# Decoder kernel: the first attention block in three-pass products with filler projections, and a new order of loading

## The reference

```
y = layernorm(layernorm(x)) * g1 + b1
q, k, v = y @ Wq + bq, y @ Wk + bk, y @ Wv + bv        # 256 -> 1024 each
g = sigmoid(y @ Wg + bg)
state_t = decay * state_(t-1) + k_t * v_t               # a scan over the 100 rows
o = (g * q * state * 64**-0.5) @ Wo + bo                # 1024 -> 256
x2 = layernorm(x) + o
h = layernorm(x2) * g2 + b2
x = x + x2 + gelu(h @ W1 + b1) @ W2 + b2                # 256 -> 1024 -> 256
```

## Time and profile before

| what | us |
|---|---|
| median of 3 runs (1713.19 to 1713.71) | 1713.41 |
| the profiled execution | 1713.2 |
| its span, first to last instruction | 1711.4 |
| PE busy | 1443.1 (84%) |
| VectorE busy | 1041.3 (61%) |
| ScalarE busy | 736.7 (43%) |
| POOL busy | 33.6 (2%) |
| mean granted TensorE clock | 0.927 |

### The profile page before, as it was taken

One profiled execution on the slowest core, in us unless ns is written; L12 is line 12 of the kernel. 1 busy time (PEld: TensorE's weight loads), 2 busy tenths in 40 slices (PEclk: granted clock), 3 DMA queues, 4 the chain that ended last, 5 costly groups with the idle time before them and its releaser, 6 DMA issues.

```text
span 1711.4 us, 26949 instructions
## 1 busy us (share of the span) xinstructions
PE 1443.1 (84%) x9474; PEld 1143.6 (67%) x9474; DVE 1041.3 (61%) x2519; ACT 736.7 (43%) x1919; POOL 33.6 (2%) x31
## 2 busy tenths in 40 slices
PE   0498989898799999999999999843899995997608
PEld 0355656565588787888888888632788885677608
DVE  4843434334466666666666666578566765687784
ACT  0322122222366555565555655510444533443744
POOL 1000000000100000000000000000000002000100
PEclk9899999999899999999999999966799996998858
DMA  9120000000000000000000000001100000220001
GB/s 298 30 99 1 0 0 0 0 0 0 17 10 10 19 10 9 9 9 9 9 9 9 9 9 1 1 0 27 43 1 0 0 0 0 73 72 1 1 0 39
DMA packets 29797, 35.56 MB, mean 21 GB/s; under 512 B 5119, under 2 KB 26928, under 8 KB 29744
## 3 DMA queue, kind: packets, MB, share of 16 engines
q1 hardware_dynamic: 27840, 27.53, 5.5%
q0 software_dynamic: 1904, 7.34, 1.3%
HBM read 33.20 MB, written 1.65 MB: 20 GB/s over the span
## 4 chain that ended last, share of the span: by engine, by line
PE 72%; DVE 17%; ACT 5%; issue 4%; DMA 1%; SPq 0%; DVEq 0%; ACTq 0%
PE bank L624 10%; PE bank L659 8%; PE bank L660 7%; PE bank L661 7%; PE bank L721 5%; PE bank L705 5%; PE bank L713 4%; PE bank L632 3%; PE bank L681 3%; PE bank L650 3%; PE bank L642 3%; PE bank L851 2%; PE bank L875 2%; ACT s L1297 2%; DVE amax L1832 2%
## 5 line engine op out<-in xcount | busy, mean ns | idle before, releaser
L1218 ACT ACTIVATE prob<-bank,nmx 100x361 f32<-100x361 f32 x256 | 142.5, 560 | 124.6 <-DVE nmx L1633 124.6
L1633 DVE TENSOR_REDUCE nmx<-bank 100x1 f32<-100x361 f32 x256 | 124.7, 528 | 44.7 <-PE bank L705 33.8
L1589 DVE TENSOR_TENSOR oTl<-bank,oTh 128x100 fp32r<-128x100 f32 x128 | 33.3, 260 | 120.1 <-ACT oTh L1204 120.1
L659 PE MATMUL bank<-cxTh,wxkh 128*128 128x362 f32 x256 | 99.1, 387 | 0.8 <-DVE kTl L1590 0.6
L721 PE MATMUL bank<-pT,vv 128*64 128x100 f32 (+1 forms) x1536 | 95.5, 260 | 0.7 <-DVE oTl L1589 0.7
L1650 DVE TENSOR_SCALAR prob<-prob,rsum 100x361 f32<-100x361 f32 x256 | 92.9, 405 | 4.5
L721 PEld LDWEIGHTS bank<-pT,vv 128*64 128x64 f32 (+1 forms) x1536 | 70.3, 138 | 35.8 <-issue 23.1
L713 PE MATMUL bank<-ident,prob 100*128 100x100 f32 (+1 forms) x768 | 89.7, 253 | 1.9 <-DVE prob L1650 1.9
L713 PEld LDWEIGHTS bank<-ident,prob 100*128 100x128 f32 (+1 forms) x768 | 84.5, 151 | 7.2 <-DVE prob L1650 2.7
L1204 ACT CAST oTh<-bank 128x100 fp32r<-128x100 f32 x128 | 31.7, 248 | 128.6 <-PE bank L721 128.6
L659 PE MATMUL bank<-wxvh,cxTh 128*128 128x512 f32 (+1 forms) x192 | 83.7, 436 | 1.0 <-DVE vv L1618 1.0
(11 more groups left out here) (342 smaller groups left out, 3598.8 us busy)
## 6 DMA issues: line engine op xcount, KB each, us to landing
cx<-in_ctx_dram SPq DMA_DIRECT2D x32, 128.0 KB, 2.1
xc<-in_ctx_dram SPq DMA_DIRECT2D x32, 128.0 KB
mask_i<-in_mask_BxS_ik_dram SPq DMA_DIRECT2D x16, 141.0 KB
w<-in_L_attn_W_dram POOLq DMA_DIRECT2D x2, 1024.0 KB, 26.9
cx<-in_ctx_dram SPq DMA_DIRECT2D x16, 105.0 KB, 2.1
xc<-in_ctx_dram SPq DMA_DIRECT2D x16, 105.0 KB
x<-in_x_dram SPq DMA_DIRECT2D x1, 1600.0 KB
out_dram<-x SPq DMA_DIRECT2D x8, 200.0 KB
```

The source lines that it names most:

```text
L659: pe.matmul(o, wh, mh, start=start, stop=False)
L1218: nc.scalar.activation(prob[:, h % 4, :], bank[S_BANKS[e]][0:T, 0:S], ACT.Exp, bias=nmx[:, h:h + 1], accum_out=psum_[:, h:h + 1]).then_inc ...
L1633: nc.vector.tensor_reduce(nmx[:, h:h + 1], bank[S_BANKS[e]][0:T, 0:S], AX_X, ALU.max, negate=True).then_inc(xa_max, 1)
```

## The change

*Loading.* SP issues x by groups of four, the four projection weights by halves of 512 columns in the order k, g, v, q, then Wo, W1, W2 and two raw weights. ScalarE's queue issues the identity, the vectors and the small ones. POOL issues no DMA any more. Later raw weights go into the same two buffers (`raw6`, `raw2`) as these come free.

*First norms.* The second of two norms without gain has the same mean, so `u0` is made from x with one factor, `rstd_z`, that is worked out from the first variance; first for group 0, the others within group 0's chunks.

*Products.* All seven weights of the block are split in high (ScalarE) and low (VectorE); POOL does both for the second halves of k, g, v, q. Rows, heads and hidden values are split too: y and h by ScalarE (whole and high) and POOL or VectorE (low), heads and gelu outputs by POOL. All products are `split_matmul`. Wo and W2 now give the transposed sum: the weights are stationary, each chunk is added to banks 4 and 5 as soon as it is split, ScalarE copies the sum with its bias, and PE transposes it back (`sums_back`). k, g, v and q have one bank each.

*Filler.* While a group's end runs, PE makes the first three chunks of the next group. `transposes(u0, SIDE_BANK0, l0_t)`, those of the second norm, stand ahead of the whole third of them.

*Side jobs.* The weight transposes of the head, and the rounding, are spread over the groups (`JOBS_AT`). The transposed FFN weights are written to HBM (`parked`) and loaded back when the 4-bit layer is done.

The loop over groups is written out. The core of the diff, PE first:

```diff
-            with pe.Fori(0, NG) as g:
-                for c in range(KC):
-                    p = 4 * (c % 2)
...
-                    for w, b in ((wk0, 1), (wg0, 3), (wv0, 2), (wq0, 0)):
-                        for k in range(KD):
-                            mm = pe.matmul(bank[p + b][:, 0:N], w[:, k, c * P:(c + 1) * P], zT[:, k, ds(N * g, N)],
...
+            def project(n, kinds):
+                c = n % KC
+                cols = slice(c * P, (c + 1) * P)
+                for kind in kinds:
+                    high, low, b, free = KINDS[kind]
+                    if c == 0 and kind == 0:
+                        pe.wait_ge(l0_z, KD * (n // KC) + KD)
+                    if n == 0:
+                        pe.wait_ge(l0_wl, kind + 1)
+                    if n == KC // 2:
+                        pe.wait_ge(l0_wb, kind + 1)
+                    if n:
+                        pe.wait_ge(free, n)
+                    for k in range(KD):
+                        mm = split_matmul(bank[b][:, 0:N], high[:, k, cols], low[:, k, cols], yTh[:, k, :], yTl[:, k, :],
...
+            for g in range(NG):
+                first, follows = KC * g, g + 1 < NG
+                for c in range(2, KC):
+                    if c > 2:
+                        project(first + c, range(4))
+                    if c == 3 and g:
+                        sums_back(2 * g - 1)
+                        heads_summed(first)
+                    if c == KC - 1 and follows:
+                        pe.wait_ge(l0_n, g + 2)
...
+                        transposes(u0, SIDE_BANK0, l0_nt)
+                    if c > 2 or g == 0:
+                        heads_summed(first + c - 2)
+                    for j in JOBS_AT.get((g, c), ()):
...
+                        side_job(j)
+                heads_summed(first + KC - 2)
+                if follows:
+                    project(first + KC, (0, 1))
+                heads_summed(first + KC - 1)
+                if follows:
+                    project(first + KC, (2, 3))
...
+                sums_back(2 * g)
+                if follows:
+                    project(first + KC + 1, range(4))
+                pe.wait_ge(l0_u, g + 1)
+                transposes(u0, SIDE_BANK0, l0_t)
+                if follows:
+                    project(first + KC + 2, range(4))
+                for c in range(KC):
+                    hidden(first + c)
+                    if c > 1:
+                        hidden_summed(first + c - 2)
+                hidden_summed(first + KC - 2)
+                hidden_summed(first + KC - 1)
```

POOL, and the end of a group on ScalarE and VectorE:

```diff
+            def split(high, low, whole, done):
+                nc.gpsimd.tensor_copy(high, whole).then_inc(pool_link, 1)
+                pool.wait_ge(pool_link, links)
+                nc.gpsimd.tensor_tensor(low, whole, high.bitcast(F32), ALU.subtract).then_inc(done, 1)
...
+            rows_low0(0)
+            pool.wait_ge(wb_in, 64)
+            for high, low, w in ((wk0h, wk0l, wk0), (wg0h, wg0l, wg0), (wv0h, wv0l, wv0), (wq0h, wq0l, wq0)):
+                split(high[:, :, 512:], low[:, :, 512:], w[:, :, 512:], l0_wb)
...
+                sums_out(g, l0_wo, "L0_attn_bo")
+                if follows:
+                    keys_gates(first + KC + 1)
                 deviation(TURN[0] + g + 1)
+                if follows:
+                    keys_gates(first + KC + 2)
                 for k in range(KD):
                     act.wait_ge(l0_t, KD * g + k + 1)
...
+                    nc.scalar.activation(full[:, k, :], src, ACT.Identity, scale=scale, bias=bias)
+                    nc.scalar.activation(hTh[:, k, :], src, ACT.Identity, scale=scale, bias=bias).then_inc(l0_hh, 1)
...
+                norm_rows(lambda t: zg[:, t, :], lambda t: u0[:, t, :], TURN[0] + g + 1).then_inc(l0_u, 1)
+                for k in range(KD):
+                    dve.wait_ge(l0_hh, KD * g + k + 1)
+                    nc.vector.tensor_tensor(hTl[:, k, :], full[:, k, :], hTh[:, k, :].bitcast(F32), ALU.subtract).then_inc(l0_h, 1)
+                if follows:
+                    gated(first + KC + 1)
+                    scanned(first + KC + 1)
+                    gated(first + KC + 2)
+                    scanned(first + KC + 2)
...
+                if follows:
+                    rows_once_normalized(g + 1)
+                    blocks_rounded((1, 2, 4)[g], (80, 96, 112)[g])
```

More of the change, by code:

```diff
@@ L129, in decoder_kernel @@
         wffn = sb("wffn", [P, KD, D], scope=late)
+        with ExitStack() as s:
+            raw6 = sb("raw6", [P, KI, D], scope=s)
+            raw2 = sb("raw2", [P, KD, D], scope=s)
         wxq = sb("wxq", [P, KD, C], scope=late)
         moments, std, rstd = moments_all[:, 0:G], std_all[:, 0:G], rstd_all[:, 0:G]
-        s0 = ExitStack()
-        z = sb("z", [T, B, D], scope=s0)
         with ExitStack() as s:
[L137 to L157, removed]
@@ L661, in split_matmul, with side_job @@
                 return pe.matmul(o, wl, mh, start=False, stop=stop)
+            def side_job(j):
+                kind, what, blocks, raw, count, need = JOBS[j]
+                o = bank[SIDE_BANK0 + j % 2]
+                if raw is not None:
+                    pe.wait_ge(raw, count)
+                if need:
+                    pe.wait_ge(prep_q, need)
+                if j > 1:
+                    pe.wait_ge(prep_c, j - 1)
+                if kind == "line":
+                    pe.wait_ge(small_in, 16 * SMALL_DMAS)
+                    pe.wait_ge(memsets, 7)
+                    mm = pe.matmul(o[0:H, 0:LINE], rel[:], onehot[:], start=True, stop=True)
+                elif kind == "product":
+                    for m in range(KD):
+                        for k in range(KD):
+                            mm = pe.matmul(o[:, m * D:(m + 1) * D], raw6[:, k, m * P:(m + 1) * P], raw6[:, 2 + k, :],
+                                           start=(k == 0), stop=(k == KD - 1))
+                else:
+                    for q in range(4):
+                        mm = pe.transpose(o[:, q * P:(q + 1) * P], blocks[q], ident[:])
+                mm.then_inc(prep_t, 1)
@@ L1118, in _ @@
[L1118 to L1130 removed]
+                        act.wait_ge(ln_t, KD * NG * (n - 1) + KD * g + k + 1)
@@ new lines, in sums_out @@
+            def sums_out(g, summed, name):
+                if summed is l0_w2:
+                    act.wait_ge(l0_es, KC * g + KC)
+                elif g == NG - 1:
+                    act.wait_ge(park_out, 16 * 3 * g)
+                for m in range(KD):
+                    act.wait_ge(summed, KD * KC * g + KD * (KC - 1) + m + 1)
+                    nc.scalar.activation(full[:, m, :], bank[SUM_BANK0 + m][:, 0:N], ACT.Identity,
+                                         bias=column(name, m)).then_inc(l0_sc, 1)
@@ L1131, in _, with job_out @@
+            def job_out(j):
+                kind, what = JOBS[j][0:2]
+                src = bank[SIDE_BANK0 + j % 2]
+                act.wait_ge(prep_t, j + 1)
+                if kind == "qk":
                     heads = lambda w: w[:, what, :].rearrange("p (h e) -> p h e", e=32)[:, :, 0:DH1]
```

796 lines of the change are left out of this document (519 added, 277 removed).

## The result

The changed kernel takes 1647.73 us (median of 4 runs, 1636.35 to 1648.9) against 1713.56 (1713.19 to 1713.94) for the kernel before: a ratio of 0.961, 95% interval 0.957 to 0.965. Two further sets of runs of the same kernel gave 1638.82 and 1639.24. Forecast were 1634 and a range of 1594 to 1672. Executions of the changed kernel fall into two groups, near 1637 and near 1648, and the last experiment shows where they part.

What follows compares the result with a forecast made beforehand. PE was taken to bound the rounds, and DMA, then VectorE, the head. The first block ending 80.7 us earlier and 1 us lost at the second attention gave 1713.2 - 80.7 + 1 = 1633.5, forecast 1634 us, range 1594 to 1672.

Steps and rivals of the forecast that it cites:

- The start: Head of the kernel: with reordered loads the first projection comes at about 22 us (bounds 19 and 30), 66 us off.
- Group 0: First four sequences: PE idles 11 us before the first head sum, behind POOL's weight splits; eighth chunk ends at 82 us.
- A full round: From one group's eighth chunk to the next's: 66 us of PE work plus waits, 81.5 us instead of 89.
- Value bank: Third filler projection: its value product waits 5 us for the bank that VectorE frees only after both low parts.
- Hidden part: FFN steps at a group's end: 17.6 us of PE, plus 4 from POOL and VectorE excluding each other (bounds 0 and 10).
- Half clock: In each round, PE's slow clock after a wait of 3 to 5 us costs 1.5 us.
- The chunks: Projection chunks: POOL's exclusion makes VectorE's work 4.6 us, hidden under PE's 5.5.
- The end: Last group, which has no filler: 17 us to the first hidden product, 17.6, then 3; with the half clock 40 us.
- The sum: End of the first block: 82+245+40 = 367 us instead of 447.7, 80.7 us earlier.
- The border: Before the second attention: nine loads of 2.3 MB ahead of the bias loads on SP cost 1 us (bounds 0 and 5).
- Rival 2: POOL bounds chunks and hidden parts: rounds of 93 us, total 1686; decided at 2.2 us of POOL a chunk; 17%.
- Rival 1: PE alone bounds the block, waits mostly covered and POOL never late: rounds of 71 us, total 1589; 25%.

Runs made afterwards that it cites:

- the last experiment: The changed kernel run again in a third set without an edit, to catch a long execution in the profile: 1639.24 us, ratio 0.957.

## Why the prediction was right

The forecast is for the profiled execution's kind, and against that it is 2 us off (1634 and 1636.35); the medians lie 5 to 14 us above it, inside the range. By its own steps:

- **The start**: 22 us predicted, 21.28 measured. x was there at 5.6 us (5 to 6 predicted), `logits` at 11.2 (10). The walk through the head is borne out by the trace. What the small loads, the loads of x, the norms and the rounding are worth each is not shown: the one run on it moved the small loads alone and won nothing, while x landed later.
- **Group 0**: eighth chunk at 82 predicted, 76.5 measured. POOL's split of the second halves is where I put it (25.7 to 41.8 us, 16 us for four; forecast 13.5 to 20), but it cost PE 5.48 us, in one wait at 40.26, and not 11: the mis-sized term of the sum. The path was another one, too. The forecast had the first head sum wait for POOL; it starts at 43.93 without a wait. What PE waited for was the value bank, and VectorE, which frees it, was late because its own steps beside POOL's were long: the first chunk's four scans 5.14 us instead of 1.13, its gating 2.61 instead of 0.58, and the subtraction for Wo 3.12 where those for W1 and W2 take 2.26 and 2.28.
- **A full round**: 81.5 predicted, 82.9, 85.5 and 86.4 measured. Products 336 a round at 0.183 us, as predicted. Value bank 5 predicted, 4.7 to 4.9 measured. Second norm 3 and 2.2. Hidden part 21 to 22 predicted, measured 22.2 in all three (107.7 to 129.9 in the first). The waits for `el` are 3.1 to 3.3 us of it, in five places; the other 1.4 over the 17.6 are no half clock (at most one product there is 0.333 apart): behind each wait the products take some 0.26 us more than its idle time until they stream again. Half clock 1.5 predicted; 19 to 21 products at 0.333 instead of 0.183 make 3. The next group's first product: 2 predicted, 1.3 measured where no store is in the way and 3.9 and 3.4 where it is. That wait was missing from the walk through the order: ScalarE shares a place between the parking copies and the rows.
- **The chunks**: the forecast let POOL lengthen VectorE's chunk from 3.1 to 4.6 us, hidden under PE. In the chunks of the rounds the scans keep their 1.13 us and the gatings theirs; it cost the sum nothing.
- **The end**: 40 predicted, 40.3 measured: 16.5 to the first hidden product (17), 21.5 for the hidden part (17.6, and 2.4 for the half clock), in which 17 products are 0.333 apart (2.6 us), and 2.3 behind it (3).
- **The sum**: 82+245+40 = 367 was 76.5+254.8+40.3 = 371.6. An error of -5.5 and one of +10 partly cancel, and that is luck: it is why the total is closer than its parts. Of the 10, about 4 are half-clock products (59 in three rounds, 8.9 us, instead of 4.5) and about 3 the store; the rest was not traced.
- **The border**: 1 us predicted, nothing measured. The bias loads are issued at 1119.8 and their product at 1128.8 waits for ScalarE's `zT`, not for them.
- **POOL on 400 columns**: cast 0.5 and subtraction 0.85 predicted, 0.52 and 1.05 measured alone. Rival 2 needed 2.8 for both; the hidden values' mean in the rounds is 0.77+1.40 = 2.17, just under its point of decision of 2.2, and in the last group, with nothing of VectorE's beside it, 1.57. The heads' split keeps 1.6. The rounds took 83 to 86 us and not the 93 of this rival. Rival 1, rounds of 71, fell by the same numbers.

The Trainium skill, "SBUF — State Buffer", section "Who interferes with whom", calls the port pair of VectorE and GpSimd an exclusive lock. The trace agrees, and beyond the rounding: while POOL subtracted 1024 columns, the four scans of a chunk (two inputs in SBUF) took 5.14 us, otherwise 1.13:

```profile
26.77 2.40 POOL L608 TENSOR_TENSOR wk0l<-wk,wk0h 128x1024 fp32r<-128x1024 f32 x1
30.31 2.39 POOL L608 TENSOR_TENSOR wg0l<-wg,wg0h 128x1024 fp32r<-128x1024 f32 x1
```

```profile
28.83 5.14 DVE L1842 TENSOR_TENSOR_SCAN state<-decay,kv 128x100 f32<-128x100 f32 x4
34.01 2.61 DVE L1846 SCALAR_TENSOR_TENSOR state<-gate,state 128x400 f32<-128x400 f32 x1
```

## What to carry to other kernels

When PE's work is cut and filled with the next group's, the gain is decided by the order on the other engines: for each filler product ask which bank it writes, who frees it, and what stands ahead of that on its engine. Here three orders written the other way round, and one step given to an engine with air, were worth 34 us beside the 75 of the change. And moving a load moves the ones behind it: when the small loads left SP's queue, `logits` landed 12.8 us earlier, x 3.5 us later, and nothing was won. Before and after such a move, look when each of the loads lands that the next instruction needs.

## What was not expected of the hardware

The same code at the same distance from a block's end, to within 3 us, on one core alone, ran either at the full or at half of TensorE's clock for 24 us with PE busy nearly throughout, in about every second execution of the changed kernel (7 of its 15 runs lie above 1645). The 43 runs of before lie between 1712.68 and 1719.33, without two groups 10 us apart. PE came to that stretch in both cases from the same softmax, with the same waits of 0.5 us (0.53 and 0.52) and 1.48 us. Which of the two an execution takes is not explained here, nor why the kernel before was spared; a comparison of medians of such kernels is good to some 5 us, and the block's own end was the better measure.
